# Four small layers with a conditioning vector: the attention's first steps with the values in a bank of their own and new orders, and in the late steps GpSimd's next input between the two normalisations

## What is computed

```python
x = L0(x, cond)      # RMS norm scaled by cond, 256 -> 2*1024, gelu gate, quantised, 1024 -> 256, residual
# L1, attention part: 16 heads of 16 features
h = gamma * x * rsqrt(mean(x*x) + 1e-6) + beta      # gamma, beta = cond @ W.T
q, k, v = split(h @ W_q.T), split(h @ W_k.T), split(h @ W_v.T)
attn = softmax(0.25 * q @ k.T, axis=-1)             # 64 x 64 per sequence and head
x = x + alpha * (join(attn @ v) @ W_o.T)
x = x + alpha2 * swiglu(rmsnorm2(x))                # L1, MLP part: 256 -> 2*1024 -> 256
x = L2(x, cond)      # adapter with weights generated from cond, 256 -> 128 -> 256
x = L3(x, cond)      # layer norm, plus tanh of a function of cond
```

## Time and profile before

| | before |
|---|---|
| median of 3 runs | 741.75 us |
| profiled execution | 741.11 us |
| its span | 739.3 us |
| PE busy | 721.8 us, 98% |
| PE weight loads | 586.4 us, 79% |
| VectorE busy | 514.7 us, 70% |
| ScalarE busy | 359.3 us, 49% |
| GpSimd busy | 410.6 us, 56% |
| TensorE's granted clock, mean | 0.998 |

### The profile page before, as it was taken

The page is one execution under the profiler, slowest core; times in us unless marked ns, Lnnn a source line. Parts: engine busy times, 40 slices in busy tenths (PEclk is TensorE's granted clock), DMA queues, the critical chain, the costliest instruction groups (busy, mean ns, idle before and its releaser), DMA issues.

```text
span 739.3 us, 18704 instructions
## 1 busy us (share of the span) xinstructions
PE 721.8 (98%) x6700; PEld 586.4 (79%) x6700; DVE 514.7 (70%) x808; ACT 359.3 (49%) x722; POOL 410.6 (56%) x408
## 2 busy tenths in 40 slices
PE   9999999999999899999999999999999999999996
PEld 8888888888888788888888777777777767778884
DVE  4977777777789989888995465656655566453466
ACT  4534444344447677888874333333333332322585
POOL 5645655554678888999997624224242423320244
PEclk9999999999999999999999999999999999999999
DMA  8854544445432000000004255577667777759943
GB/s 301 258 111 99 108 121 101 100 111 121 110 73 63 22 28 17 17 1 0 1 4 134 104 173 175 177 220 216 191 190 251 212 215 231 238 160 390 386 178 142
DMA packets 81339, 106.25 MB, mean 144 GB/s; under 512 B 39904, under 2 KB 53376, under 8 KB 81152
## 3 DMA queue, kind: packets, MB, share of 16 engines
q1 hardware_dynamic: 79840, 103.34, 46.7%
q10 hardware_dynamic: 1440, 2.11, 1.1%
HBM read 75.77 MB, written 21.27 MB: 131 GB/s over the span
## 4 chain that ended last, share of the span: by engine, by line
PE 75%; POOL 16%; issue 5%; DVE 3%; ACT 1%; DMA 0%; POOLq 0%; DVEq 0%; SPq 0%; ACTq 0%
PE banks L446 24%; PE banks L1317 22%; PE banks L1347 12%; POOL p_sb L1047 5%; PE banks L1369 4%; PE banks L530 4%; POOL mlp_in L182 2%; PE banks L1979 2%; PE banks L1949 2%; POOL mlp_in L186 2%; POOL x_sb L1056 2%; POOL att_in_lo L191 1%; PE banks L1971 1%; POOL mlp_in L188 1%; PE banks L548 1%
## 5 line engine op out<-in xcount | busy, mean ns | idle before, releaser
L629 ACT ACTIVATE gelu<-banks,rstd 128x512 f32<-128x512 f32 x64 | 44.0, 688 | 115.8 <-PE banks L446 114.1
L1699 DVE TENSOR_TENSOR g<-banks,silu 128x512 f32<-128x512 f32 x64 | 44.2, 690 | 77.6 <-PE banks L1317 44.9
L1703 DVE TENSOR_TENSOR g_lo<-g,g_hi 128x512 fp32r<-128x512 f32 x64 | 55.7, 870 | 47.6 <-ACT g_hi L1539 47.6
L1539 ACT ACTIVATE g_hi<-g 128x512 fp32r<-128x512 f32 x64 | 40.4, 631 | 96.0 <-DVE g L1699 95.0
L1533 ACT ACTIVATE silu<-banks 128x512 f32<-128x512 f32 x64 | 38.2, 597 | 97.4 <-PE banks L1317 97.4
L446 PE MATMUL banks<-up_hi,xs_hi 128*128 128x512 f32 x254 | 81.1, 400 | 0.0
L446 PE MATMUL banks<-up_hi,xs_lo 128*128 128x512 f32 x256 | 79.2, 391 | 0.0
L1317 PE MATMUL banks<-mlp_in_hi,w_hi 128*128 128x512 f32 x252 | 78.8, 394 | 0.0
L446 PE MATMUL banks<-up_lo,xs_hi 128*128 128x512 f32 x256 | 78.8, 390 | 0.0
L1317 PE MATMUL banks<-mlp_in_lo,w_hi 128*128 128x512 f32 x252 | 78.0, 390 | 0.0
L1317 PE MATMUL banks<-mlp_in_hi,w_lo 128*128 128x512 f32 x252 | 77.8, 390 | 0.0
(11 more groups left out here) (230 smaller groups left out, 1736.2 us busy)
## 6 DMA issues: line engine op xcount, KB each, us to landing
gen_hyper<-in_gen_t SPq DMA_DIRECT2D x32, 512.0 KB, 4.4
gen_made<-base_w SPq DMA_DIRECT2D x64, 256.0 KB, 4.4
adapter_w<-gen_made SPq DMA_DIRECT2D x64, 256.0 KB, 4.4
tokens<-in_x_tok SPq DMA_DIRECT2D x32, 128.0 KB, 2.3
w_stage<-in_w_t SPq DMA_DIRECT2D x32, 128.0 KB, 2.6
tokens_again<-in_x_tok SPq DMA_DIRECT2D x32, 128.0 KB, 2.2
weight_slot<-adapter_w SPq DMA_DIRECT2D x4, 1024.0 KB, 8.8
x_sb<-in_x_t SPq DMA_DIRECT2D x7, 512.0 KB, 6.3
```

The costliest lines, as they stand in the source:

```text
L629: nc.scalar.activation(gelu[:, j, :], up_bank(s, j, 1)[:, :], ACT.Gelu, scale=rstd0[:, bass.ds(s.at(0), 1)]).then_inc(Z["gelu_done"], 1)
L1539: nc.scalar.activation(gs[0][:, f % 2, :], g[:, f % 2, :], ACT.Copy).then_inc(S["g_hi_done"], 1)
L1699: nc.vector.tensor_tensor(g[:, f % 2, :], chunk_bank(s, f, 1)[:, :], silu[:, f % 2, :], ALU.mult).then_inc(S["g_done"], 1)
L1703: nc.vector.tensor_tensor(gs[1][:, f % 2, :], g[:, f % 2, :], gs[0][:, f % 2, :].bitcast(FP32), ALU.subtract).then_inc(S["g_ready"], 1)
```

## The change

In the attention's first steps the values get bank 0 in every step, with a wait for the bank's reader, the scaled output (`ya_done`), or in steps 2 and 3 for the copies of the values before. The keys of a step wait for the copied keys of the step before. The output product, which uses bank 0 too, now waits in every step from 4 on for the value copies of its own step (`v_low_done`, `v_high_done` of tile t-2). VectorE copies values only in the first step that has any and for the last tile, so that ScalarE makes all four copies in steps 3 to 8 as it does in the late ones. PE's sums of squares go behind keys and queries. In step 3 ScalarE copies the queries ahead of the second exponential. GpSimd takes both normalisations ahead of the low part in step 3, and in step 4 the order normalisation (0), low part, normalisation (1), residual. From step 8 on the first multiplication of the next input stands between the two normalisations. The number of matrix products, DMAs and other operations is the same; nothing moves on the DMA queues.

```diff
@@ -926,7 +926,7 @@
             return rows.rearrange("p (n b) (g e f) -> p b e n g f", b=2, e=2, f=HD)[:, member, parity]
 
         def value_sums(s, member, parity):
-            rows = bank[0 if s.first_tile(2) or s.first_tile(3) or plain(s) else 1][L * member:L * (member + 1), :]
+            rows = bank[0][L * member:L * (member + 1), :]
             return rows.rearrange("p (n g e f) -> p e n g f", n=2, e=2, f=HD)[:, parity]
 
         def pair_of(ap, two):
@@ -946,7 +946,7 @@
             return not isinstance(s.t, int) or s.t >= PEELED
 
         def vector_takes_values(s):
-            return not plain(s) or s.last(2)
+            return s.first_tile(2) or s.last(2)
 
         def rows_live(s):
 
@@ -1057,6 +1057,7 @@
 
             def attention_body(s):
                 following = Step(s.t + 1, s.k + 1, NA, s.turns)
+                first_two = s.first_tile(3) or s.first_tile(4)
                 if s.live(0):
                     if not plain(s):
                         attention_input(nc, pool, core, s, 0)
@@ -1065,17 +1066,22 @@
                         first["row_scales"](pool, e35)
                     if plain(s):
                         residual(s)
+                    if first_two:
+                        normalise(s, 0)
                     if s.first_tile(3):
-                        normalise(s, 0)
+                        normalise(s, 1)
                     wait(pool, A["v_ready"], s.at(1) if s.live(2) else 0)
                     attention_input(nc, pool, core, s, 2)
+                    if s.first_tile(4):
+                        normalise(s, 1)
                     if not plain(s):
                         residual(s)
-                if not s.first_tile(3):
+                if not first_two:
                     normalise(s, 0)
-                normalise(s, 1)
                 if before_plain(s) and following.live(0):
                     attention_input(nc, pool, core, following, 0)
+                if not first_two:
+                    normalise(s, 1)
 
             def generator_base():
                 pool.wait_ge(A["base_loaded"], 32)
@@ -1169,26 +1175,24 @@
             def keys(s):
                 if s.live(1):
                     pe.wait_ge(A["h_ready"], s.at(1) + 1)
-                    if s.first_tile(3):
+                    if s.live(2):
                         pe.wait_ge(A["k_done"], s.at(1))
-                    elif s.live(2):
-                        pe.wait_ge(A["v_low_done"], s.at(1))
-                        pe.wait_ge(A["v_high_done"], s.at(1))
                     project(s, W1_K, bank[1], "k_ready")
 
             def values(s):
 
                 if not s.live(1):
                     return
-                k, apart = s.slot(1, 2), s.first_tile(1) or s.first_tile(2) or before_plain(s)
-                if before_plain(s):
+                k = s.slot(1, 2)
+                if s.live(4):
                     pe.wait_ge(A["ya_done"], s.at(4) + 1)
-                elif not apart:
-                    pe.wait_ge(A["k_done"], s.at(1) + 1)
+                elif s.live(2):
+                    pe.wait_ge(A["v_low_done"], s.at(1))
+                    pe.wait_ge(A["v_high_done"], s.at(1))
                 for pair in range(2):
                     for n, (a, b) in enumerate(SPLITS):
                         for d in range(DH):
-                            last = nc.tensor.matmul(bank[0 if apart else 1][:, pair * D:(pair + 1) * D],
+                            last = nc.tensor.matmul(bank[0][:, pair * D:(pair + 1) * D],
                                                     ha[a][k][:, d, pair * P:(pair + 1) * P],
                                                     w1[b][:, W1_V + d * D:W1_V + (d + 1) * D],
                                                     start=n == d == 0, stop=n == 2 and d == DH - 1)
@@ -1271,7 +1275,7 @@
                 if s.live(4):
                     ps = output_ps(s)
                     pe.wait_ge(A["ot_done"], s.at(4) + 1)
-                    if plain(s) and not s.last(3) and not s.last(4):
+                    if not s.last(3) and not s.last(4):
                         pe.wait_ge(A["v_low_done"], s.at(2) + 1)
                         pe.wait_ge(A["v_high_done"], s.at(2) + 1)
                     wait(pe, A["ya_done"], s.at(4))
@@ -1288,9 +1292,9 @@
                 transposes(s, 0)
                 output(s)
                 transposes(s, 1)
-                squares(s)
                 keys(s)
                 queries(s)
+                squares(s)
                 weighted_values(s)
                 if s.first_tile(4):
                     pe.wait_ge(A["sub_done"], PAIRS * s.at(2) + 1)
@@ -1508,10 +1512,10 @@
                 exponentials(s, 0)
                 first_two = s.first_tile(3) or s.first_tile(4)
                 take_transposed(s, 1)
+                if s.first_tile(3):
+                    take_queries(s)
                 if first_two:
                     exponentials(s, 1)
-                if s.first_tile(3):
-                    take_queries(s)
                 if s.live(0):
                     wait(act, A["v_ready"], s.at(1) if s.live(2) else 0)
                     attention_input_high(nc, act, core, s.at(0), s.slot(0, 2))
```

## The result

| | before | changed |
|---|---|---|
| median, 6 runs each | 741.73 us (741.10 to 741.99) | 746.16 us (743.98 to 746.83) |
| ratio | | 1.0057, 95% interval 1.0046 to 1.0068 |
| profiled execution, span | 741.11, 739.3 | 746.83, 744.2 |
| TensorE's mean clock in it | 0.998 | 0.991 |

What follows compares the result with a forecast made beforehand. GpSimd's dates in the attention were taken to bound the kernel, carried to the end one for one. Profiled 741.11 + 1.35 (early) + 0 (late) = 742.5; median 0.64 above, so 743.1; range 740.8 to 745.6.

Steps and rivals of the forecast that it cites:

- the early part: Attention's early steps, from step 3 on: +1.35 together, with step 4's late residual reaching GpSimd in step 5.
- The square's wait: ScalarE's square of the first tile waits over 4 for GpSimd's residual, starting at 258.26 instead of 255.28.
- The gap: PE stands 4.7 before step 5's output, from 255.7 to 260.42, waiting for all four value copies.
- The late order: GpSimd's next first multiplication between the normalisations: 0 counted; -1.6 if GpSimd alone set the pace.
- The mechanism named: Late steps: the softmax loop, 9.89 a step against GpSimd's 9.95, and the later second normalisation absorb the gain.
- Rival A: TensorE's clock halves in step 5's gap: 2.4 to 3.4 on top of 1.35, time 745.5 to 746.5; chance 0.15.
- the forecast's case: Whole kernel: early steps +1.35, late steps 0, median 743.1; bounds +1.0 to +1.9, chance 0.45.
- The wait's terms: Early attention: -0.74 in steps 3 and 4, then step 5's low part +1.26, some 0.08 in step 6; together +1.35.
- Steps 3 and 4, first half: First normalisation 0.90 earlier, step 4's input -0.74; ScalarE's two further copies lie in its 0.82 wait for the keys.
- Step 5: Output starts 2.61 late behind the value copies; GpSimd's low part at 264.50 instead of 263.25, +1.26.
- Steps 6 to 8: ScalarE's high copy some 0.08 late once more in step 6; in time in steps 7 and 8, GpSimd leading.
- Late steps: Steps 9 to 15: 0 net; GpSimd's first normalisation of step 15 at 368.45 instead of 367.10, again +1.35.

Runs made afterwards that it cites:

- the filled kernels: The change plus 17 products of ones on PE in step 5's gap before the output: 743.94 us; with 6 more in step 4: 744.06 us.
- the kernel with 17 and 6 products: The change plus 17 products of ones on PE ahead of step 5's output and 6 ahead of step 4's first transposes: 744.06 us, 1.0035.

## Why the prediction was wrong

**Right:** the early part is where the time goes, the residual behind both normalisations is the cause (with the square out of its way 3.6 of the 4.4 are gone, with GpSimd's old orders all of it), and it acts through the square and the four copies on step 5's output. The square's wait was to be over 4 and is 4.58. The gap was to be 4.7 and is 4.70, but that is partly luck: with the start taken off it runs from 256.59 to 261.29 and was forecast from 255.7 to 260.42, so both ends are 0.9 late. The late order was costed at 0, and both kernels that isolate it show 0. The mechanism named holds in the loop (scores still 9.9 apart, 0.3 gained and not 1.6); that the sum is 0 is luck, since the last tile loses 0.7, which I had not looked at.

**The step that failed is the clock.** The sum ran the output, the transposes and all behind them at 1.00, and the fall was a rival with 0.15. I let the one fall that the trace before shows, after 4.1 of idleness at the end of the run, stand for the idleness that it takes, and added that it might not come after the same time elsewhere only as an argument against. It came 1.9 into the gap. The Trainium skill (TensorE: Matmul & The Clock Gate, Part 1) says the array falls to half rate once it has been idle; the trace agrees, with 0.50 from 259.1 to 266, and I had it beside the rival instead of in the sum. Rival A was priced at 2.4 to 3.4 above the forecast's case; the filled kernels show 1.9 to 2.2. It is smaller because output and transposes took 1.6 more (3.93 against 2.32) and not 2.4, and the keys behind ran at full clock again from 266.

**The wait's terms were too small, together by 0.85 to 1.25.** Without the clock the change was to cost 1.35 and costs 2.2 to 2.6. By the kernel with 17 and 6 products, whose clock stays up, with 0.11 of start taken off:

- Steps 3 and 4, first half: -0.38 instead of -0.74. ScalarE's two further copies did not lie in its wait of 0.82. They pushed the first layer's last copy (line 620) from 234.80 to 236.37 in the changed kernel, and PE's first transposes of step 3 wait for it (`x_done`): these started at 236.85 against 235.87, 0.33 later with the start taken off, where I had left them in place. VectorE's first subtraction, which had not waited for them, now does, for 0.53. The values behind them gained 0.45 of the 0.71, and the second transposes 0.45 of the 0.6 to 0.7. The first normalisation gained 0.59 instead of 0.90, which is 0.31 of the 0.36. The wait of 1.75 before step 4's transposes was missed too. PE comes to it 1.1 earlier than before, and the low part of the weighted values, which queues behind VectorE's second sum, comes only 0.1 earlier: the transposes start at 244.73 with the start taken off, against 244.81. With the exponential ahead of the queries they start at 244.21.
- Step 5: the low part is 1.74 late (265.10) instead of 1.26; 0.35 of the 0.48 is the term above.
- Steps 6 to 8: 0.3 more, as step 8's low part waits 1.15 for the high copy instead of 0.87; I had 0.08. It does so in the two kernels with GpSimd's old orders too and not with the late order alone, so it belongs to the values apart with their copies.
- Late steps: 2.08 late at step 8 and 1.84 in step 15, so the loop gives back 0.24; at the last tile it is 2.56. There the normalisation waits 2.2 to 2.3 for its reciprocal in every kernel with the late order, and 1.58 before. The kernels with that order and no loss lose as much: they end no later because they come to the last tile 0.3 to 0.85 ahead. Why the late order makes the last tile wait was not looked into.

These are dates of one execution each, while the 2.2 to 2.6 are from medians.

**The range** left out the upper half of A, at 745.6. A with its lower price, 745.5, lay inside; the 1 us that the wait's own terms were short by took the result over the edge. That 746.16 lies within A's 745.5 to 746.5 is two errors that offset: the clock priced too high, the wait too low.

## What to carry to other kernels

When an edit opens a gap on TensorE in a stage that it almost fills, put the fallen clock into the sum and not among the rivals, and read the granted clock of every stretch before trusting a duration. Ask of every instruction moved back who is first in the queue of the engine that waits for it: the square was needed by nobody soon, but it stood ahead of four copies on which PE's next product hung. Look at the last tile too: an order that pays in the loop can cost as much where the loop runs out. And an idle share of an engine in a pipeline with two loops of nearly equal length (9.95 and 9.89, or 10.62 and 10.6) is worth only the difference.

## What had not been expected of the hardware

The clock fell after idleness much shorter than at the end of the run: in the changed kernel's step 4 PE had stood for 1.75 before 245.38 (it fell at about 245.5), in the kernel with the square behind the high copy 2.04 before 262.49, and it fell while PE was already at work again (0.63 over 264 to 268 with PE busy all of the 4.00). In the kernel with the exponential first again, PE was busy for 2.80 of 4.00 between 244 and 248 with no wait over 0.8, and the clock was 1.00; it also stayed at 1.00 after that kernel's wait of 1.57 before 256.88. In the kernel with GpSimd's old orders it came about 1.7 after PE was back (transposes at 244.71; the clock by windows of 1 us).

```profile
245.00:246.00 1.00, 1.00 (x19) 0.93 (x15) 0.96 (x2) 0.54 (x1) 1.00 (x2) 1.00 0.00 0
246.00:247.00 1.00, 1.00 (x8) 1.00 (x8) 1.00 (x2) 0.61 (x2) 1.00 (x1) 0.69 0.00 0
247.00:248.00 1.00, 1.00 (x15) 0.78 (x15) 0.97 (x1) 0.93 (x1) 1.00 (x2) 0.50 0.00 0
```

And the same wait does not always bring the fall. Eight of the profiled kernels stand 1.74 or 1.75 before step 4's transposes. In five the clock fell, 0.1 to 1.7 after PE was back; in the other three (the residual ahead, and the two with the square moved) it stayed at 1.00. The kernel with the square behind the high copy:

```profile
243.92 0.71 PE L1241 MATMUL banks<-ident,p_sb 64*128 64x64 f32 x16 [1.75 <-DVE ot_lo L1671]
```
```profile
244.00:248.00 4.00, 4.00 (x54) 3.73 (x55) 3.93 (x4) 2.96 (x4) 3.78 (x4) 1.00 0.00 0
```

The waits of 2.04 and more in step 5 (2.04, 2.86, 3.22, 4.69 and 4.70) brought it in each of the five profiles that have one.

The same gap also seems not to cost the same in each run: the kernel with the residual ahead lies between 741.30 and 745.31 in 12 runs, the one with only the values apart between 741.36 and 742.47 in 11. In those 12 the three with the lowest mean clock, 0.993, took 743.37 to 745.31 and the six with 0.996 or more 741.30 to 743.84, which fits a clock that falls in some runs and not in others. It is a hint only: the mean also holds the end of the run, and the kernel before itself spreads over 2.3 in 23 runs.
